# Order of the mask of equal sources and the look-up of kinds in the gate rows of a graph kernel, and where slot numbers are read

## The reference

```python
gate = jax.nn.silu(edge_attr @ F1W + F1b) @ F2W + F2b
ei = emb[atom_z[src]]
ej = emb[atom_z[dst]]
gate = gate + (ei * (ej @ adapt)).sum(-1, keepdims=True)
...
msg = gate * h[dst] * (cw * mj)[:, None]
agg = jax.ops.segment_sum(msg, src, num_segments=N)
...
smax = jax.ops.segment_max(score, src, num_segments=N)
```

## Time and profile before

| what | value |
|---|---|
| median of 3 runs | 8639.19 us (8637.67 to 8662.36) |
| the profiled execution, its own time | 8656.44 us |
| its span in the trace | 8654.4 us |
| gate pass, first comparison of sources to the last instruction of its rows | about 2431 to 3937 us |
| mean granted TensorE clock, whole span | 0.891 |
| busy share over the span: PE, PEld, DVE, ACT, POOL | 79%, 71%, 69%, 53%, 64% |

### The profile page before, as it was taken

One profiled execution on the slowest core, in us unless ns is written; L12 is line 12 of the kernel. 1 busy time (PEld: TensorE's weight loads), 2 busy tenths in 40 slices (PEclk: granted clock), 3 DMA queues, 4 the chain that ended last, 5 costly groups with the idle time before them and its releaser, 6 DMA issues. The chain is left out here.

```text
span 8654.4 us, 298124 instructions
## 1 busy us (share of the span) xinstructions
PE 6795.9 (79%) x145772; PEld 6115.4 (71%) x92150; DVE 5987.6 (69%) x15859; ACT 4585.8 (53%) x14638; POOL 5516.6 (64%) x7877
## 2 busy tenths in 40 slices
PE   6445455555468888885999889997999799987998
PEld 6344444444368888884888778886888688877998
DVE  6566666666568888887888778877888688863111
ACT  0122222222157777774888668885888588870000
POOL 2277777777756666663888678884888588870000
PEclk9877777777789999996999799997999699988999
DMA  9522222222157777772777367763777277745565
GB/s 388 221 81 73 81 78 73 81 78 76 62 180 231 234 231 232 235 234 100 236 237 236 106 214 235 232 200 118 234 234 233 78 239 234 234 160 219 242 249 212
DMA packets 703404, 1590.72 MB, mean 184 GB/s; under 512 B 91156, under 2 KB 394852, under 8 KB 697535
## 3 DMA queue, kind: packets, MB, share of 16 engines
q1 hardware_dynamic: 643378, 1489.78, 50.7%
q0 software_dynamic: 52768, 77.90, 2.9%
q10 hardware_dynamic: 5869, 3.84, 0.1%
HBM read 1151.49 MB, written 419.69 MB: 182 GB/s over the span
## 5 line engine op out<-in xcount | busy, mean ns | idle before, releaser
L1919 ACT ACTIVATE vals<-carry_h,weight 128x49 f32<-128x49 f32 x9604 | 2320.6, 326 | 6.6
L939 POOL DMA_INDIRECT edge_records<-rec_space,slot_all x1600 | 1572.5, 983 | 723.0 <-issue 482.1
L422 PE MATMUL psum<-TT,hd_t 128*128 128x97 bf16 x9604 | 1380.5, 208 | 139.5 <-DMA hs_t<-one_hots 132.8
L416 PE MATMUL psum<-TT,hd_t 128*128 128x97 bf16 x19208 | 1444.7, 208 | 0.0
L422 PEld LDWEIGHTS psum<-TT,hd_t 128*128 128x128 fp8e4 x9604 | 938.7, 98 | 441.0 <-issue 151.9
L1964 POOL TENSOR_TENSOR vals<-vals 128x343 f32<-128x343 f32 x1372 | 1070.8, 780 | 92.9
L1959 POOL TENSOR_TENSOR vals<-vals 128x343 f32<-128x343 f32 x1372 | 1042.0, 760 | 4.7 <-ACT vals L1919 4.7
L1824 DVE SCALAR_TENSOR_TENSOR xks<-recs,psum 128x343 f32<-128x343 f32 x1372 | 695.8, 507 | 358.7 <-PE psum L416 343.7
L416 PE MATMUL psum<-ts,hs_t 128*128 128x49 bf16 x19208 | 922.0, 184 | 0.0
L822 PE MATMUL psum<-ident,hot_bs 125*128 125x125 bf16 x800 | 133.4, 257 | 998.1 <-DVE look L896 979.6
L822 PEld LDWEIGHTS psum<-ident,hot_bs 125*128 125x128 bf16 x800 | 91.5, 117 | 1160.5 <-issue 1152.8
(11 more groups left out here) (348 smaller groups left out, 16244.3 us busy)
## 6 DMA issues: line engine op xcount, KB each, us to landing
AJ<-adjacency SPq DMA_DIRECT2D x35, 5488.0 KB, 16.7
recs<-attributes SPq DMA_DIRECT2D x196, 686.0 KB, 5.5
hs<-one_hots SPq DMA_DIRECT2D x392, 336.0 KB, 3.2
one_hots<-hots SPq DMA_DIRECT2D x343, 336.0 KB, 4.2
edge_records<-zeros SPq DMA_DIRECT2D x49, 2278.5 KB, 20.8
recs_g<-edge_records SPq DMA_DIRECT2D x343, 325.5 KB, 5.2
recs<-attributes SPq DMA_DIRECT2D x196, 514.5 KB, 3.7
hd_t<-one_hots SPq DMA_DIRECT2D x196, 448.0 KB, 4.7
```

The source lines that it names most:

```text
L416: return e.add_instruction(mybir.InstMatmult(name=nc.get_next_instruction_name(), engine=mybir.EngineType.PE, ldweights=False, start_tenso ...
L422: e.matmul(out, hot, parts[0], start=True, stop=False)
L939: e.indirect_dma_start(REC[:, :], bass.IndirectOffsetOnAxis(ap=slot_all[:, i % SR, s:s + 1], axis=0), rec_rings[:, (i // 2) % 4, s, i % 2, ...
L1919: last = e.activation(vals[:, c, 0, :], carry_h[:, par(back), c, :], ACT.Copy, scale=weight[:, par(back), c:c + 1])
```

## The change

Three lines change. On PE, `make_same` of group g-1 comes ahead of `look_up_kinds` of group g-2. On ACT, `take_same` of g-1 comes ahead of `copy_src` of g-2. On DVE, the slot numbers in `mark_filled` and `mark_empty` are read from `iota_p` in PSUM and no longer from `iota_f` in SBUF.

```diff
@@ PE
-                    stages([(1, flip_src), (5, scatter_group), (1, make_adj), (2, rank), (3, look_up_nodes), (1, flip_dst), (2, look_up_kinds), (1, make_same)])
+                    stages([(1, flip_src), (5, scatter_group), (1, make_adj), (2, rank), (3, look_up_nodes), (1, flip_dst), (1, make_same), (2, look_up_kinds)])
@@ DVE
-                    slot = iota_f[:, 0:KS].unsqueeze(1).broadcast_to([P, NB, KS])
+                    slot = iota_p[:, 0:KS].unsqueeze(1).broadcast_to([P, NB, KS])
@@ ACT
                     stages([(1, take_hot(0, src_flipped, src_bytes, src_taken)), (1, take_adj), (1, take_dst),
-                            (2, copy_src), (1, take_same)])
+                            (1, take_same), (2, copy_src)])
```

## The result

| | before | changed |
|---|---|---|
| median | 8646.67 us (8637.67 to 8662.36, 4 runs) | 8575.83 us (8558.53 to 8581.29, 4 runs) |
| profiled execution, span | 8654.4 us | 8579.2 us |
| a row of the gate pass (first to last L1474, over 48) | 30.43 us | 28.98 us |

The ratio is 0.9907 with a 95% interval of 0.9894 to 0.9919: 70 to 92 us faster, 71 by the medians. I had forecast 131 us and a time of 8508 (8460 to 8555). The direction was right; the time lies above the range and the gain is about half. The row came out 1.2 us longer than the 27.8 us forecast.

The account below looks back on a forecast made before the run. The gate pass was taken as bound by a ring of waits, with no engine full. 172 us from the PE and ACT edits less 41 us of DVE's backlog gave 131 us, a median of 8508 us (8460 to 8555).

Parts of the forecast that it names:

- PE and ACT edits: Gate pass: mask ahead of kinds shortens the turn from 4.28 to 3.78 us, 172 us over 343 groups.
- The new wait of the mask for the adjacency: PE's mask load waits for ACT's adjacency copy, 0.16 us a turn, some 50 us in the list of waits.
- DVE's backlog: DVE's extra work once a row makes `pair_up` late and stops PE by about 0.84 us a row, 41 us.
- Slots: DVE's slot comparisons, read from PSUM, take 0.56 us each; worth 28 us over the pass.
- the other 0.47 us is scattered, and I keep it: Gate pass row: 30.43 us less seven turns of 29.96, kept unchanged in the forecast row of 27.8 us.
- third rival: Gate pass: no change within measurement (8639), as another ring, DMA the candidate, is 4.28 us too; chance 0.04.
- Rival 1: POOL's branch in the gate pass has more room: turn 3.77 us, 160 us gained, 8479; chance 0.22.
- rival 2: DVE's slot change does nothing and the backlog is paid in full: 103 us gained, 8536; chance 0.09.
- the slower rival: ACT's `take_adj` waits for a late adjacency store, holding all groups: at 0.8 us lateness 103 us slower, 8742; chance 0.04.
- critical ring: Gate pass: waits between PE and ACT, from one `make_adj` load to the next, set the turn of 4.28 us.

Follow-up runs that it names:

- e3: The changed kernel with ACT's old list, so only PE's list and the slots differ from the kernel before: 8744.13 us, ratio 1.0114 to the kernel before.
- e5: The changed kernel with POOL's list reordered, `rest` and `third` ahead of `add_pairs`: 8547.50 us, ratio 0.9892 to the kernel before.
- e13: The changed kernel with one piece of DVE's row work, L1479, moved two turns later: 8556.63 us, ratio 0.9889 to the kernel before.
- e1: The changed kernel with slot numbers read from SBUF as before, so only the two reordered lists: 8583.25 us, ratio 0.9925 to the kernel before.
- e2: The kernel before with only the slot numbers read from PSUM, in the old order: 8646.80 us, ratio 1.0003 to the kernel before.
- e11: The kernel before with 21 more one-column products in each group on PE, ahead of `flip_src`: 8767.99 us, ratio 1.0124 to the kernel before.
- e7: The changed kernel storing fewer one-hots and attributes from the second row on, output not the reference's: 8531.99 us, ratio 0.9856 to the kernel before.

## Why the prediction was wrong

**PE and ACT edits: right.** 172 us were forecast from a turn of 3.78 us; turns of 3.73 and 3.81 are in the trace, and the six ordinary turns of a row come to 3.80 us each (mean of the medians by place). The new wait of the mask for the adjacency showed on the load side only. In the kernel before, the load of `flip_dst` in the turn of the earlier trace rows is

```profile
2603.18 0.27 PEld L1378 LDWEIGHTS psum<-pack,hots_dst 128*128 128x128 fp8e4 x7
```

0.21 us ahead of the kinds; in the changed kernel it is 0.31 us ahead of the mask, so the wait is 0.10 of the 0.16 us forecast. The some 50 us that I wanted to see in the list of waits are 0.2 us there, since the products ahead of it still ran. e3 shows that PE's list alone does harm.

**DVE's backlog: right in size, though in two stops.** 0.84 us a row or 41 us were forecast, and the long turn of the row is 4.62 us, 0.84 above 3.78. The list of waits shows less of it (28.5 us in 1360), as it counts idle time only from the modelled end of the products before. There were two stops in that turn, for DVE and then for POOL, where I had charged one; e5 and e13 each take one of them away. That the sum agrees to the last digit is in part luck, since the first stop was not in it.

**Slots: right duration, the value overstated.** 28 us were forecast. e1 gives 13 us by the turns and 16 by the ratios, the latter within the noise, and e2 nothing without the reordering, as stated. I had charged 0.3 us for each comparison; the first cost the turn 0.05 us and the second 0.27.

**The step that failed** is the sentence "the other 0.47 us is scattered, and I keep it". I had 30.43 us a row against seven turns of 29.96 and took the difference as a constant of the pass. Most of it was PE's issue stalls (15.3 us in 1360, or 0.34 us a row), and they are no constant: 4.0 us in 1360 at a turn of 4.60 (e3), 15.3 at 4.28, 70.5 at 3.78. In the changed kernel a row is 28.98 us and its undisturbed turns 27.43, so what I had kept at 0.47 us is 1.55, and the stalls in the list are 1.50 of it. The turns themselves, forecast as 7 x 3.78 + 0.84 = 27.30 us, are 0.13 off. Together that is the 1.2 us by which the row came out longer, 59 us over the pass; 131 - 59 = 72 us, against 71 by the medians and 80 by the ratio. My third rival had looked at the DMA queues only as a data rate and a mean ("0.72 of its time busy"), and so missed both the queue that carries instructions and the bursts.

Rival 1 was wrong (PE does wait for POOL once a row), and so was rival 2 (the slots got faster). The third did not come true as written (the time fell), and the slower rival did not occur: `take_adj` waited for PE, as before. The forecast and rivals 1 and 2 add up to a chance of 0.92, where the text has 0.88.

What stays open: where in a busy DMA system the start of a packet of instructions is held; how the 107 us of e11 divide; and how far a smoother order of SP's queue could bring the remaining 45 to 65 us down.

## What to carry to other kernels

When a wait on the critical ring is removed, what was slack for everything else goes too: look at once-a-row work, at idle time ended by "issue", and at the queues behind them, and ask what each costs at the new rate. A mean DMA share says nothing of bursts; a store in the issuing queue that waits long for one late producer delays all behind it and then releases them together, and placing it where its data are surely ready was worth 37 us here, more than either change to DVE's or POOL's list (16 and 13 us). Order changes on two engines that hand a buffer to each other belong together: PE's alone cost 98 us here (with the slots from PSUM), both gained 65 (e1), and 80 with the slots.

## What the runs showed of the hardware

PE's instructions came in packets of 16.4 KB, one for 246 recorded products and loads, through queue q8. At 44 instructions a microsecond (59559 in 1360 us) late packets left PE idle for up to 2.5 us at a time, and each such time ended 1.15 to 1.62 us after a packet had landed; in the kernel before, at 42 (62398 in 1501 us), the stalls were about a fifth as much (15.3 against 70.5 us), and with 48 a microsecond in the same old order (e11: 76428 in 1590 us) as much as in the changed kernel. With small stores (e7) PE did 46 a microsecond (62231 in 1360 us) with 20.0 us of stalls. A packet took about 1.0 us whether it came late or not.

A VectorE comparison of 392 elements with both operands in SBUF took 865 ns at the median, where GpSimd was mostly at work, 561 at the least (L1474), and 555 with one operand in PSUM; a GpSimd copy that met it took up to 761 ns against 421. The Trainium skill ("SBUF — State Buffer", section "Who interferes with whom") says that a VectorE instruction with two SBUF inputs and a GpSimd instruction that reads SBUF exclude each other, and that one with at most one SBUF input, outside the modes that use both of its ports, does not contend; the runs agree in both directions. The 62 cycles more for a PSUM source, from the table of the Trainium skill ("VectorE: DVE Perf Modes", section on the TRN2 errata) that I weighed against the edit, did not show: 555 ns from PSUM against 561 from SBUF.
